# Second dense layer of a gated cross-attention stack: its steps placed among those of the attentions on either side

## What is computed

```python
x = x + g * L0_xattn(layernorm(x), ctx);  x = x + g * L0_ffn(layernorm(x))   # 8 experts, capacity 128
x = x + g * L1_xattn(layernorm(x), ctx);  x = x + g * L1_ffn(layernorm(x))   # dense, the layer of this change
x = x + g * L2_xattn(layernorm(x), ctx);  x = x + g * L2_ffn(layernorm(x))   # shared + 16 experts
x = x + g * L3_xattn(layernorm(x), ctx);  x = x + g * L3_ffn(layernorm(x))   # 4 experts

def L1_ffn(h):                     # 704 hidden features, weights in {-1, 0, 1} with scales
    gate = (h @ gate_w.T) * gate_s
    up   = (h @ up_w.T) * up_s
    return ((silu(gate) * up) @ down_w.T) * down_s
```

## Time and profile before

| what | value |
| --- | --- |
| median of 3 runs | 1230.61 us (1228.82 to 1235.83) |
| the profiled execution, its own time | 1231.18 us |
| its span, first to last instruction | 1229.4 us |
| TensorE busy (matmul) | 951.7 us, 77% |
| VectorE busy | 655.6 us, 53% |
| ScalarE busy | 438.9 us, 36% |
| GpSimd busy | 386.6 us, 31% |
| mean granted TensorE clock | 0.875 |
| chain that ended last | PE 56%, DVE 17%, issue 9%, POOL 6%, DMA 5%, ACT 3% |

### The profile page before, as it was taken

How to read it: one execution, slowest core, us unless ns; L and a number is a source line. 1 busy time by engine, 2 the same in 40 slices (tenths; PEclk the granted TensorE clock), 3 DMA queues, 4 the chain that set the end, 5 groups by cost and what they waited for, 6 DMA issues and landing times.

```text
span 1229.4 us, 18893 instructions
## 1 busy us (share of the span) xinstructions
PE 951.7 (77%) x6616; PEld 563.7 (46%) x6616; DVE 655.6 (53%) x1548; ACT 438.9 (36%) x721; POOL 386.6 (31%) x519
## 2 busy tenths in 40 slices
PE   4899973588279899577557953899989998289993
PEld 1455542577234346455326731244444444146562
DVE  5778844143479424277652336978888862311111
ACT  1466651111036420354312410165656666022220
POOL 5223215312443001344122024156565656200002
PEclk9999996788679899799678975599999999589997
DMA  6344515363634000644144832101040001710002
GB/s 181 113 114 149 192 43 202 125 221 124 193 95 122 29 1 1 180 93 103 39 167 130 240 107 79 40 2 40 2 142 3 1 3 36 303 39 22 18 14 78
DMA packets 112700, 116.32 MB, mean 95 GB/s; under 512 B 58824, under 2 KB 102408, under 8 KB 109576
## 3 DMA queue, kind: packets, MB, share of 16 engines
q1 hardware_dynamic: 101760, 96.62, 25.6%
q10 hardware_dynamic: 7776, 10.10, 2.5%
q0 software_dynamic: 3072, 8.39, 2.2%
HBM read 88.17 MB, written 30.67 MB: 97 GB/s over the span
## 4 chain that ended last, share of the span: by engine, by line
PE 56%; DVE 17%; issue 9%; POOL 6%; DMA 5%; ACT 3%; SPq 2%; another core or an unknown queue 1%; POOLq 0%; DVEq 0%; ACTq 0%
PE psT L1179 7%; PE psT L1330 7%; PE psT L1478 6%; PE psB L1294 4%; DVE mxp L1871 4%; PE psO L1362 4%; PE psO L1374 3%; PE psB L1492 3%; DVE mxp L1875 3%; PE psB L1179 3%; PE psB L1300 3%; PE psB L1543 2%; PE psT L1441 2%; PE psB L1519 2%; PE psO L1364 2%
## 5 line engine op out<-in xcount | busy, mean ns | idle before, releaser
L1871 DVE TENSOR_REDUCE mxp<-psB 128x1 f32<-128x512 f32 x256 | 163.8, 684 | 37.3 <-PE psB L1294 36.6
L1330 PE MATMUL psT<-whole 99*128 99x256 bf16 (+2 forms) x1024 | 152.8, 275 | 19.1 <-issue 18.5
L1875 DVE TENSOR_REDUCE mxp<-psB 128x2 f32<-128x512 f32 x192 | 123.6, 685 | 30.1 <-PE psB L1300 29.7
L1630 ACT ACTIVATE Pt<-psT,ln 128x1024 f32<-128x1024 f32 x96 | 106.7, 1114 | 63.7 <-PE psT L1330 62.6
L1330 PEld LDWEIGHTS psT<-whole 99*128 99x128 bf16 (+2 forms) x1024 | 96.7, 101 | 62.2 <-issue 27.8
L1630 ACT ACTIVATE Pt<-psT 128x1024 f32<-128x1024 f32 x96 | 98.1, 1024 | 56.9 <-PE psT L1330 55.2
L2202 POOL TENSOR_TENSOR rstd<-vare,cst 128x1 f32<-128x1 f32 x64 | 35.7, 559 | 256.0 <-DVE vare L1789 255.7
L1294 PE MATMUL psB<-whole 96*128 96x512 bf16 x256 | 95.9, 426 | 24.6 <-DMA whole<-scr_q 14.3
L1300 PE MATMUL psB<-whole 96*128 96x256 bf16 x384 | 77.9, 305 | 35.6 <-DMA whole<-scr_q 22.3
L1478 PE MATMUL psT<-whole,qf 128*128 x176 | 82.2, 611 | 0.6 <-ACT qf L1680 0.6
L2259 POOL TENSOR_SCALAR nb_t<-Pt 128x1024 f16<-128x1024 f32 x64 | 67.4, 1052 | 39.1 <-ACT Pt L1630 37.0
(11 more groups left out here) (309 smaller groups left out, 1759.1 us busy)
## 6 DMA issues: line engine op xcount, KB each, us to landing
whole<-in_w SPq DMA_DIRECT2D x32, 512.0 KB, 4.7
whole<-in_w SPq DMA_DIRECT2D x5, 3072.0 KB, 10.3
xn<-scr_sorted ACTq DMA_DIRECT2D x42, 128.0 KB, 2.2
scr_q<-sq SPq DMA_DIRECT2D x48, 96.0 KB
whole<-scr_q SPq DMA_DIRECT2D x24, 192.0 KB
whole<-scr_k SPq DMA_DIRECT2D x24, 192.0 KB, 3.5
scr_sorted_out<-xn SPq DMA_DIRECT2D x31, 128.0 KB, 2.6
scr_k<-sk SPq DMA_DIRECT2D x32, 96.0 KB, 1.9
```

The costliest lines, as they stand in the source:

```text
L1330: ins = pe.matmul(psT[:, s.n % 2, i * A.T:(i + 1) * A.T], lhsT=k_at[:, h * kw + s.c * P:h * kw + (s.c + 1) * P], rhs=q_at[:, h * A.T:(h + ...
L1630: act.activation(p_slot(A, s.p)[:, 0:4 * A.T], psT[:, s.n % 2, 0:4 * A.T], ACT.Exp, bias=bias, scale=scale).then_inc(T_used[s.n % 2], 1)
L1871: dve.tensor_reduce(mxp[:, s.un.g % 2, at:at + 1], psB[:, s.n % BANKS, :], AX.X, ALU.max).then_inc(bank_used[s.n % BANKS], 1)
L1875: dve.tensor_reduce(mxp[:, s.un.g % 2, at:at + 2], psB[:, s.n % BANKS, :].rearrange("p (h n) -> p h n", h=2), AX.X, ALU.max).then_inc(bank ...
```

## The change

The twelve `gu` and eight `down` steps of the second dense layer become thunks with due times. Both barriers go.

- The six `gu` steps of token group 0 are merged into the second attention, at 11.35, 11.675, 12.0, 12.325, 12.65 and 12.975.
- All others are merged into the third attention: `down` of group 0 at -0.95, -0.75, -0.55, -0.35; `gu` of group 1 at -0.9, -0.517, -0.133, 0.25, 0.633, 1.017; `down` of group 1 at 1.5, 1.7, 1.9, 2.1. Each `down` is followed by its `stats`.
- A `gu` step waits for the `xt` of the last batch of its own group only (checked at chunk 0).
- The hidden buffer moves to the upper halves of the QP slots (group 0) and of the KP slots (group 1), which attentions 1 and 2 leave free. Silu's result goes to `nb_t`, which the third attention uses for its clipped scores.
- The loads of items 9 and 10 both follow the last `down` in the list, at 2.1 in the third attention. Item 10 waits for that `down`.
- VectorE's extra waits before `down` and `stats` on all evacuations are left out for this layer.

```diff
+FFN1 = (11.35, 13.3, -0.95, 1.5, -0.9, 1.4)
...
     def attention(A, later, before):
-        if A.layer == 2:
-            barrier()
         add("attn_begin", A=A)
...
+    def gate_up1(tg, ch):
+        blk = ffn_blocks(1)[0]
+
+        def f():
+            xt = [s for s in steps if s.kind == "xt" and s.xn.b == tg * 4 + 3][-1]
+            assert xt.layer == 1
+            last["T1", tg] = add("gu", layer=1, blk=blk, tg=tg, ch=ch, width=blk.widths[ch], h=tg, m=xt.m,
+                                 n=take("T"), sg=take("sg")).n
+        return f
+
+    def down1(tg, tc):
+        blk = ffn_blocks(1)[0]
+
+        def f():
+            s = add("down", layer=1, blk=blk, tg=tg, tc=tc, h=tg, last_T=last["T1", tg], n=take("S"))
+            stats(tg * 4 + tc, s.n)
+            item_free[blk.item] = s.n
+            if tg == 1 and tc == 3:
+                wload(9)
+                wload(10)
+        return f
+
+    def ffn1_first():
+        n = len(ffn_blocks(1)[0].widths)
+        return [(gate_up1(0, ch), FFN1[0] + (FFN1[1] - FFN1[0]) * ch / n) for ch in range(n)]
+
+    def ffn1_rest():
+        n = len(ffn_blocks(1)[0].widths)
+        return [(down1(tg, tc), FFN1[2 + tg] + 0.2 * tc) for tg in range(2) for tc in range(4)] \
+            + [(gate_up1(1, ch), FFN1[4] + (FFN1[5] - FFN1[4]) * ch / n) for ch in range(n)]
...
-        before = (moe_capacity, lambda: dense(1), sorted_pairs, sorted_experts)[i]()
+        before = (lambda: moe_capacity() + ffn1_first(), ffn1_rest, sorted_pairs, sorted_experts)[i]()
...
-        def hidden(layer):
-            return Hb if layer == 1 else Hb2
+        def hidden(layer, h, ch):
+            if layer == 1:
+                at = 6144 * h + 2048 * (ch // 2) + 1024 + 512 * (ch % 2)
+                return arena[:, at:at + 512]
+            return Hb2[:, h % 2, ch, :]
+
+        def silu_slot(layer, i):
+            return nb_t[:, i % 2, :] if layer == 1 else sg[:, i % 2, :]
...
                     if s.after is not None:
-                        for i in range(BANKS):
-                            if s.after[i]:
-                                dve.wait_ge(bank_used[i], s.after[i])
+                        evacuated(dve, s.after)
...
-                    for i in range(BANKS):
+                    for i in range(BANKS if s.layer == 2 else 0):
                         if s.x_after[i]:
                             dve.wait_ge(bank_used[i], s.x_after[i])
```

More of the change, by code:

```diff
@@ L648, in sorted_pairs @@
             + [(gather(b), -0.005 if b < 6 else 0.1) for b in range(2, NB)]
+    def gate_up1(tg, ch):
[23 more added lines that the diff above has]
+            + [(gate_up1(1, ch), FFN1[4] + (FFN1[5] - FFN1[4]) * ch / n) for ch in range(n)]
     def dense(layer):
-        if layer == 1:
-            barrier()
         blocks = ffn_blocks(layer)
@@ L657, in down @@
             blk, tg, h, last_T = work
-            final = blk is blocks[-1]
             for tc in range(4):
@@ L661, in down @@
                 s = add("down", layer=layer, blk=blk, tg=tg, tc=tc, h=h, last_T=last_T, x_after=x_after, n=take("S"))
-                if final and layer == 1:
-                    stats(tg * 4 + tc, list(s_count))
             h_free[h] = s.n
             s_last[0] = item_free[blk.item] = s.n
[L666 to L669, removed]
         xt_last = [s.m for s in steps if s.kind == "xt"][-1]
@@ L682, in dense @@
         down(pending)
-        return s_last[0] if layer == 2 else []
+        return s_last[0]
     before = []
@@ L1542, in _ @@
                     for ch, w in enumerate(s.blk.widths):
-                        ins = pe.matmul(psB[:, s.n % BANKS, 0:256], lhsT=hidden(s.layer)[0:w, s.h % 2, ch, s.tc * P:(s.tc + 1) * P],
+                        ins = pe.matmul(psB[:, s.n % BANKS, 0:256], lhsT=hidden(s.layer, s.h, ch)[0:w, s.tc * P:(s.tc + 1) * P],
                                         rhs=W[0:w, off + ch * 256:off + (ch + 1) * 256], start=(ch == 0), stop=(ch == last))
@@ L1703, in _ @@
                     sc = col("gs1", s.ch, w) if s.layer == 1 else 1.0
-                    act.activation(sg[0:w, s.sg % 2, :], psT[0:w, s.n % 2, 0:512], ACT.Silu, scale=sc
+                    act.activation(silu_slot(s.layer, s.sg)[0:w, :], psT[0:w, s.n % 2, 0:512], ACT.Silu, scale=sc
                                    ).then_inc(silu_done, 1)
@@ L2147, in _ @@
                     up = psT[0:w, s.n % 2, 512:1024]
-                    dst = hidden(s.layer)[0:w, s.h % 2, s.ch, :]
+                    dst = hidden(s.layer, s.h, s.ch)[0:w, :]
                     if s.layer == 1:
                         ins = dve.scalar_tensor_tensor(out=dst, in0=up, scalar=col("us1", s.ch, w),
-                                                       in1=sg[0:w, s.sg % 2, :], op0=ALU.mult, op1=ALU.mult)
+                                                       in1=silu_slot(s.layer, s.sg)[0:w, :], op0=ALU.mult, op1=ALU.mult)
                     else:
-                        ins = dve.tensor_tensor(dst, up, sg[0:w, s.sg % 2, :], ALU.mult)
+                        ins = dve.tensor_tensor(dst, up, silu_slot(s.layer, s.sg)[0:w, :], ALU.mult)
                     ins.then_inc(T_used[s.n % 2], 1)
```

1 line of the change is left out of this document (removed).

## The result

The changed kernel took 1213.2 us in the median of four runs (1210.56 to 1216.19), beside 1230.62 us for the kernel before (1228.82 to 1235.83). The ratio is 0.985, with a 95% interval of 0.981 to 0.990. By the ratio that is 18.2 us less; the two medians lie 17.4 us apart. The forecast was 1212 in a range of 1206 to 1223.

The account below looks back on a forecast made before the run. TensorE bounds the dense layer; around it, barriers turn two chains of waits into idle PE time. Savings of 24.8 us less 1.4, 0.5, 2 and 1.5 paid give 19.4 us, from 1231.18 to 1212 us, range 1206 to 1223.

Parts of the forecast that it names:

- (a): Tail of the second attention: its 6.02 us, with little PE work, is covered by gate/up steps; 4.2 us saved.
- (b): First gate/up matmuls: they no longer follow an idle PE, so lose nothing to the lower clock; 2.2 us saved.
- (c) and (d): Behind the last down, the 3.16 us gap goes, 3.2 us; from front 0's fx to front 2's, 12.6 us go.
- (f): Ahead of down(0,0): PE waits for the last chunk's Silu and product, hidden before by group 1's gu; 1.4 us paid.
- (h): Dense layer's long groups mixed with short attention groups: PE idle time, between 0 and 6.2 us, taken as 2 us paid.
- (e): From front 2's fx to the evacuation of its fq: PE no longer slowed by preceding idle time; 2.6 us saved.
- (g): Front 0's chain, third attention: 12.95 us of PE work covers 13.4 us from fq 0 to st; 0.5 us paid.
- (i): Loads of items 9 and 10 ahead of front 2's store and pack: delay of 0 to 13 us, taken as 1.5.
- The slow clock: Rival, chance 0.05: the new 77 us stretch, cut by short waits, runs at a lowered PE clock; up to 1241 us.
- The gain given back: Rival, chance 0.06: the third attention's 19.2 us loop is tied to something other than front 2; 1229 us.
- Thin cover: Rival with mixing, chance 0.17: front 0's chain is served late behind gu work, 5 us more; together 1221 us.
- The load in front: Rival, chance 0.10: items 9 and 10 push front 2 back by 13 us instead of 1.5; 1223 us.

Follow-up runs that it names:

- e1: The changed kernel's code with the dense layer's steps in the old order between the attentions, barriers and extra waits gone; 1229.59 us, ratio 0.9963 to the kernel before.
- e5: The change with down of group 0 due from -0.89 instead of -0.95, so gu(1,0) goes ahead of down(0,0); 1210.66 us, ratio 0.9816 to the kernel before.
- e6: The change with all gate/up steps of group 1 due before front 0's fx, leaving less matmul work beside its chain; 1218.41 us, ratio 0.9881 to the kernel before.
- e9: e5 with the loads of items 9 and 10 at 7.75, behind all fronts of the third attention; 1207.7 us, ratio 0.9784 to the kernel before.
- e7: The change with the loads of items 9 and 10 at 2.7, behind front 2's stores; 1216.12 us, ratio 0.9871 to the kernel before.
- e4: The changed kernel itself, run again; 1211.51 us beside 1233.06 for the kernel before, ratio 0.9838.
- e8: e5 with group 1's downs spread to 1.5, 2.35, 3.0 and 3.6, among the first bodies; 1219.05 us, ratio 0.9895 to the kernel before.
- e10: e9 with group 1's downs at 1.5, 1.7, 3.62 and 5.62; 1208.91 us, ratio 0.9802 to the kernel before.
- e11: e8 with down(1,1) at 2.46, behind split 2 on GpSimd's queue, and the loads at 7.75; 1209.76 us, ratio 0.9806 to the kernel before.
- e2: The change with only group 0's gate/up overlapping the second attention, all else of the dense layer inline in the old order; 1223.94 us, ratio 0.9929 to the kernel before.

## Why the prediction was right

The forecast held in size and in mechanism, with one sentence to put right: "the two barriers turn both chains into idle PE time". e1 has no barriers and keeps the 9.40 us ahead of body 0; it is the order of the steps that leaves PE idle there. The markers that it named came: `fx` 2 near 496 (495.62), body 2 near 514 (513.37), clock 1.00 up to body 1, no PE break over 0.5 us but the one ahead of down(0,0) (the only other is 0.52), and the rest as long as before (695.3 and 695.8 us). At body 2, 22.4 us are gained locally where the sum had 19.4; the terms one by one:

- **(a) and (b), 4.2 and 2.2 us.** From P to the first long gate/up group passed 7.39 us and now pass 2.32 (418.16 to 420.48), with two short groups of 0.22 us moved behind it: about 4.6. The 12 gate/up groups take some 42.1 us in the chain for 44.11: 2.0.
- **(c) and (d), 3.2 and 12.6 us.** The idle time went as said. With (a) and (b) against (f) to (h), 18.3 us were forecast at `fx` 2 and 20.9 came.
- **(e), 2.6 us, was too high.** From `fx` 2 to the evacuation of fq 2 on ACT it took 5.62 us and now 4.08: 1.5. PE is no longer slow there, but the evacuation is held back by VectorE's order, which the prediction had costed at nothing. Timeline of VectorE, then of ScalarE:

```profile
495.73 0.42 DVE L2188 TENSOR_TENSOR tmp<-psB,rows 128x256 f32<-128x256 f32 x1 [1.23 <-PE psB L1570]
...
497.47 0.69 DVE L1932 TENSOR_SCALAR nb_t<-psT 128x512 f32<-128x512 f32 x1
```

```profile
498.32 0.81 ACT L1651 ACTIVATE Pt<-nb_t,att_b,att 128x512 f32<-128x512 f32 x1 [1.84 <-DVEq L1936]
...
499.20 0.62 ACT L1616 ACTIVATE kf<-psB,cols 128x128 f32<-128x128 f32 x2
...
499.70 0.63 ACT L1616 ACTIVATE qf<-psB,colx 128x128 f32<-128x128 f32 x2
```

  DVE works at down(1,3) from 495.73 and only then at the clip that the next exponential needs; ACT waits 1.84 us for it, and the evacuations of front 2 stand behind that exponential.
- **(f) 1.4 and (g) 0.5 us** measured 1.39 and 0.52. From the end of fq 0 at 471.32 to `st` at 484.77 are 13.45 us, for 13.4 by the old rows. e5 and e6 show that both terms are what they were taken for: move the order by one step, and the first goes (half of it comes back ahead of gu(1,0)); take the cover away, and the second becomes 6.8.
- **(h), 2 us, was too high.** Mixing groups of 3 us with short ones cost next to nothing: PE is idle for 0.04 us in the window of 21.70 us and for 0.00 in that of 10.85, and the three gate/up groups right behind a down take 3.63 us in the chain in place of 3.44. The row that the upper bound came from, the second attention's steady part, seems to owe its idle time to chains between its short groups; that was not tried.
- **(i), 1.5 us, was too high** in the change, where it measured nothing: 4.15 us from store to pack, the same as in e9 without the load (3.91 in the kernel before). The step that failed is "because SP's own order leaves most of the load ahead of the store": when the store was issued, some 7 of the load's 10.1 us had passed. Free mixing was not the reason, as e7 shows, and the store's landing was not on the chain.

The misses cancel in part, which is luck: (h), (i) and (a) together gave 3.9 us more than said, (b) and (e) 1.3 less; the small rest lies in (c) and (d). The profiled executions differ by 20.6 us and not by 22.4, because P itself was 2.2 us later in that of after. The ratios gave 18.2 and 20.0 us (e4), and the intervals of both hold 19.4.

**The rivals.** The slow clock fell: 1.00 over all 77 us. The Trainium skill's warning (TensorE: Matmul & The Clock Gate, A second HAM failure mode: psum-queue depth-cycling) did not apply; this trace shows groups that cycle through the banks with PE 97% busy (75.32 of 77.46 us) and no fall. The gain given back fell: the 695 us behind body 2 stayed. Thin cover fell in the change, though e6 shows what its price would be. The load in front fell in the change, but it was the right fear: with the loads some 20 us later (e7, e8) PE waits 6.31 and 7.49 us at body 3.

**What e1 gains.** e1, which keeps the old order and drops the barriers and extra waits, gains 4.6 us by the ratio and 2.7 locally, where 3.2 were forecast. The 2.7 are all found in the timelines: 0.9 because the first gate/up group waits for the `xt` of its own token group only (it starts 6.51 us behind P in place of 7.39), 0.9 because gate/up takes 43.2 us in place of 44.11, and 0.8 from the shorter gap ahead of `fx` 0 (2.32 for 3.16 us).

**What stays open.** Whether moving the loads to the end gains anything over e5, and what down(1,3) ahead of the clip on VectorE costs by itself: e8 and e10 move that down away, but there front 2 runs at a lower clock.

## What to carry to other kernels

A long block of matmuls between two phases that are bound by hand-overs is cover. Price its spreading by the idle time of the chains on both of its sides (here 3.9, 3.2 and 10.3 us), plus the clock that the idle time takes from the matmuls behind it (5.3); dropping the barriers and waits alone brought 2.7 (e1). Lay the block's pieces between a chain's last matmul and the matmul that waits for its end: count that chain on its own (13.4 us) and check that the pieces are as long. Then walk through every in-order queue that a moved step touches: here a `stats` ahead of a split on GpSimd made a store 5 us late, five VectorE instructions ahead of a clip made ScalarE wait 1.8 us, and a 3 MB load 2 us ahead of a 96 KB store made body 3 wait 6.3. Then ask whether the delay reaches PE: the late store in e8 did not delay body 2, as e11 shows.

## What was not expected of the hardware

The same code ahead of P took 412.40 to 424.04 us in profiled executions whose kernels do not differ there, and the granted clock goes with it. The stretches of 50 to 100 and 350 to 400 us in e1 (P 424.04), then in e11 (P 412.40):

```profile
50.00:100.00 50.00, 43.91 (x367) 24.11 (x365) 34.43 (x85) 27.32 (x44) 12.31 (x23) 0.90 0.42 124
350.00:400.00 50.00, 43.87 (x356) 21.84 (x356) 40.28 (x98) 26.73 (x38) 16.30 (x38) 0.85 0.39 107
```

```profile
50.00:100.00 50.00, 44.53 (x418) 25.85 (x410) 39.16 (x93) 31.10 (x49) 17.09 (x32) 1.00 0.42 125
350.00:400.00 50.00, 46.88 (x423) 24.12 (x420) 43.04 (x108) 29.73 (x44) 13.97 (x31) 0.97 0.37 101
```

Up to 11.6 us, more than half of the gain, can lie in such stretches in one execution. Distances from a common point of the trace made the parts of this change measurable to some 0.5 us, where the interval of a ratio is 6 to 11 us wide. And after the same 2.32 us without matmuls the clock was full in e1 and at its lower level in e2: the length of the last gap alone did not decide it.
